# Two images on the 128 partitions and X as the stationary operand of the convolution, with the table's rows reordered by a permuted identity

## The reference, cut to what matters

```python
xn = (x - mean) / sqrt(var + 1e-5)                   # per image and channel
y = conv(xn, conv_w, padding=15, rhs_dilation=5)     # 32 channels -> 1, 7 x 7
imp = sigmoid(gelu(batchnorm(y + conv_b)))
xs = xn * imp
idx = sort(top_k(imp.reshape(B, -1), 192))           # pixels
tokens = xs[:, :, idx].T + make_pos[idx]
t1 = layernorm(tokens + attention(tokens, 8 heads))
t2 = layernorm(t1 + relu(t1 @ w1.T) @ w2.T)
xs[:, :, idx] = t2.T
return x + xs
```

## Time and profile before

| | us |
|---|---|
| median of 3 runs | 1159.79 |
| lowest, highest | 1157.36, 1163.17 |
| span of the profiled execution, first to last instruction | 1225.6 |

### The profile page before, as it was taken

How to read it: one execution, slowest core, us unless ns; L and a number is a source line. 1 busy time by engine, 2 the same in 40 slices (tenths; PEclk the granted TensorE clock), 3 DMA queues, 4 the chain that set the end, 5 groups by cost and what they waited for, 6 DMA issues and landing times.

```text
span 1225.6 us, 21628 instructions
## 1 busy us (share of the span) xinstructions
PE 971.3 (79%) x6440; PEld 762.4 (62%) x6440; DVE 835.0 (68%) x2114; ACT 774.3 (63%) x1899; POOL 631.8 (52%) x851
## 2 busy tenths in 40 slices
PE   3986865689888988898889889986786786488676
PEld 2765643577667766776678667865664565366544
DVE  5345776488558967896879677976694676455644
ACT  2545644486547786877688768875866575267543
POOL 4333316632665368546854576557516655562352
PEclk8998988799879999999899999998987589699855
DMA  9998977555566989898989888965453555436778
GB/s 244 314 264 227 272 210 180 146 159 157 133 156 184 266 217 237 236 291 208 233 238 274 228 238 227 265 187 143 132 169 98 132 154 151 123 98 195 212 221 269
DMA packets 176252, 247.82 MB, mean 202 GB/s; under 512 B 65512, under 2 KB 71912, under 8 KB 176136
## 3 DMA queue, kind: packets, MB, share of 16 engines
q1 hardware_dynamic: 167944, 244.03, 71.9%
q0 software_dynamic: 8192, 2.40, 1.5%
HBM read 124.53 MB, written 121.80 MB: 201 GB/s over the span
## 4 chain that ended last, share of the span: by engine, by line
PE 38%; DVE 20%; ACT 12%; issue 9%; DMA 9%; another core or an unknown queue 6%; POOL 5%; SPq 1%; ACTq 0%; DVEq 0%; POOLq 0%
PE cv L527 10%; PE sc L646 7%; PE pp L659 4%; PE xb L511 4%; PE tr L561 3%; DVE res L1350 3%; ACT wgt L843 3%; PE ib L574 2%; ACT pr L872 2%; PE ms L675 2%; DMA table<-xt 2%; DMA X<-in_x 2%; DVE stats L1126 2%; DMA tok_pos<-in_pos,idx 2%
## 5 line engine op out<-in xcount | busy, mean ns | idle before, releaser
L527 PE MATMUL cv<-X,w_conv 128*128 128x330 f32 (+1 forms) x1024 | 302.2, 422 | 11.6 <-issue 5.9
L527 PEld LDWEIGHTS cv<-X,w_conv 128*128 128x128 f32 x1024 | 193.3, 203 | 45.9 <-issue 12.1
L843 ACT ACTIVATE wgt<-ib,eps_col,mom 128x440 f32<-128x440 f32 (+1 forms) x256 | 177.6, 701 | 46.3 <-DVE res L1350 22.0
L1145 DVE TENSOR_SCALAR_CACHE_REDUCE junk<-flat,th 128x379 bf16<-128x379 f32 x200 | 120.6, 603 | 115.3 <-ACT th L829 89.3
L511 PE MATMUL xb<-cst,X 128*110 128x128 f32 x900 | 153.7, 297 | 48.8 <-ACT xt L809 28.3
L646 PE MATMUL sc<-k_b,qm 128*128 128x192 f32 x768 | 172.2, 353 | 16.2 <-DVE pixf L1245 7.3
L1046 POOL TENSOR_SCALAR res<-res,mom 128x440 f32<-128x440 f32 (+1 forms) x152 | 96.0, 634 | 171.0 <-DVE res L1350 169.3
L1350 DVE SCALAR_TENSOR_TENSOR res<-tr,mom,wgt 128x440 f32<-128x440 f32 (+1 forms) x192 | 122.2, 641 | 71.4 <-PE tr L561 31.0
L809 ACT COPY xt<-xb 110x512 f32<-110x512 f32 x225 | 131.6, 585 | 58.9 <-PE xb L511 30.7
L872 ACT ACTIVATE pr<-sc,least 128x192 f32<-128x192 f32 x384 | 137.1, 415 | 31.0 <-DVE least L1314 18.6
L659 PE MATMUL pp<-cst,pr 128*96 128x128 f32 x768 | 122.5, 284 | 33.6 <-ACT pt L883 25.4
(11 more groups left out here) (170 smaller groups left out, 1534.2 us busy)
## 6 DMA issues: line engine op xcount, KB each, us to landing
table<-xt SPq DMA_DIRECT2D x240, 224.0 KB
rt<-table SPq DMA_DIRECT2D x240, 224.0 KB
out<-res SPq DMA_DIRECT2D x320, 137.5 KB
X<-in_x SPq DMA_DIRECT2D x64, 412.5 KB, 6.4
X<-in_x SPq DMA_DIRECT2D x64, 343.8 KB, 6.5
conv_rows<-cvr SPq DMA_DIRECT2D x64, 188.0 KB
y<-conv_rows SPq DMA_DIRECT2D x64, 165.4 KB
out<-res SPq DMA_DIRECT2D x64, 68.8 KB
```

Of the source, the lines that this page charges most:

```text
L527: last = mm(cv[:, 0:CUT[half]], w_conv[:, 4 * q + z], X[:, m % XI, at0:at0 + CUT[half]], start=z == 0, stop=z == 3)
L843: last = A(wgt[:, n % 2, at0:at0 + w], ib[:, at0:at0 + w], ACT.Identity, scale=mom[:, NB * g + b, 2:3], bias=eps_col[:, 1:2])
```

## The change

Two images share the partitions: partition 64*b + 2*c + s holds channel c of image b, and of each ten rows of the image the five with s. A pair has 55 tiles without padding in 14 units (V), the last of three tiles; a group is two pairs, 28 units. Each load brings one block of five rows for all 128 partitions, 11 a pair; X holds three pairs. The transposes into the table take `halves_apart`, an identity with its columns permuted, as the moving operand, so that the rows come out with the two strips apart. The convolution makes a tile of X stationary and moves the taps: for each row r of five, 11 products with up to 2 x 7 x 8 columns add into one bank; ScalarE copies the 308 columns into zs with a stride of five. Seven products for each image with shifted identities then sum the taps, so DRAM, y7 and VectorE's sum are left out. Statistics need no move between partitions: two products with two columns each, one averaging the neighbouring partitions of a channel and one permuting the result, go through bank ib. The output ring has 8 blocks of five tiles, rt holds six units instead of seven. The slot constants are new. The rest of the layer is as before but for small moves in the order.

```diff
-    U = 30
-    RQ, BLKS, BW = 30, 6, 5 * H
-    XI, RT, RING = 4, 7, 40
+    PAIRS, TILES, BLKS, BW = 2, 55, 11, 5 * H
+    V = 14
+    U = PAIRS * V
+    XI, RT, RING = 3, 6, 8
-        LOAD, INTO, MOMENTS, NORMAL = -21, -11, -5, (-2, -1, -1)
-        TAPS, SUM = (10, 17, 25, 31), (15, 20, 28, 32)
-        GELU, IMP_OUT, FLAT, SEARCH, IMP_IN = 33, 35, 38, 40, 58
...
-        EMBED, PROJECT, SCORES = 82, 86, 87
-        MIX, NORM, FEED, NORM2 = 114, 115, 118, 120
-        SCATTER, BACK, IMPB = 122, 127, (123, 127, 135, 142)
+        LOAD, INTO, STATS, AVERAGE, TURN, NORMAL = -28, -15, -16, -4, 1, (-2, -1, 1, 3, 5)
+        LAST, GELU, IMP_OUT, FLAT, SEARCH, IMP_IN = 10, 26, 28, 31, 33, 51
...
+        EMBED, PROJECT, SCORES = 75, 79, 81
+        MIX, NORM, FEED, NORM2 = 108, 109, 111, 113
+        SCATTER, BACK, IMPB = 115, 120, (116, 120, 128, 134)
         SLOTS = range(INTO, U * G + BACK + 2)
...
+            if m >= XI and k == 0:
+                eng.wait_ge(conv_ok, upto(conv_ok, (m - XI) // PAIRS, 6 * ((m - XI) % PAIRS) + 4))
+            eng.dma_start(X[:, m % XI, BW * k:BW * k + BW], x_rows[m][:, :, k]).then_inc(x_in[m % XI][k >= CUT_IN], 16)
...
-                for r in range(4):
-                    b, k = divmod(4 * u + r, RQ)
-                    last = nc.tensor.transpose(bank[0:H, 128 * r:128 * r + 128], X[:, (NB * g + b) % XI, H * k:H * k + H], ident)
+                for r in range(count):
+                    k = first + r
+                    last = nc.tensor.transpose(bank[0:H, 128 * r:128 * r + 128], X[:, m % XI, H * k:H * k + H], halves_apart)
...
-                for z in range(first, last_z):
-                    blk_in = 2 * q + z
-                    pe.wait_ge(xn_ok, upto(xn_ok, g, 3 * b + blk_in // 2))
-                    at0 = BW * blk_in + CUT[0] * half
-                    last = mm(cv[:, 0:CUT[half]], w_conv[:, 4 * q + z],
-                              X[:, m % XI, at0:at0 + CUT[half]], start=z == 0, stop=z == 3)
+                bank = cv[0:H, 0:2 * ZC].rearrange("p (a t) -> p a t", t=TB)
+                for q in range(6, BLKS) if late else range(6):
+                    lo, hi = max(0, 2 * q - 3), min(TB, 2 * q + 5)
+                    at0 = H * (5 * q + r)
+                    last = mm(bank[:, :, lo:hi], X[:, m % XI, at0:at0 + H], w_conv[:, :, lo + 3 - 2 * q:hi + 3 - 2 * q],
+                              start=q == 0, stop=q == BLKS - 1, skip_group_check=True)
...
+            def conv_last(g, h, b):
+                if b == 0:
+                    pe.wait_ge(cv_cp, upto(cv_cp, g, 6 * h + 4))
+                for k in range(KS):
+                    last = mm(cv[0:H, H * b:H * b + H], zs[:, b, k, :], shift[:, 5 * k:5 * k + H], start=k == 0, stop=k == KS - 1)
...
+            def average(g, h):
+                pe.wait_ge(stat_ok, upto(stat_ok, g, h))
+                for sem, value in ib_read[-1:]:
+                    pe.wait_ge(sem, value)
+                ib_read.append((avg_rd, upto(avg_rd, g, h)))
+                mm(ib[:, MOM:MOM + 2], pair_avg, own_mom[:], start=True, stop=True).then_inc(avg_ok, 1)
...
+                for sem, value in ib_read[-1:]:
+                    pe.wait_ge(sem, value)
+                ib_read.append((wgt_ok, upto(wgt_ok, g, u)))
+                mm(ib[:, 0:H * count], bones[:], imp_b[:, H * first:H * (first + count)], start=True, stop=True).then_inc(ib_ok, 1)
...
+                if r < 5:
+                    nc.scalar.copy(zs[:].rearrange("p b k (t r) -> p (b k) t r", r=5)[:, :, :, r],
+                                   cv[0:H, 0:2 * ZC].rearrange("p (a t) -> p a t", t=TB)).then_inc(cv_cp, 1)
...
+                if r == 0:
+                    pool.wait_ge(var_ok, upto(var_ok, g, h))
+                    gp.tensor_tensor(mom[:, m, 2:3], mom[:, m, 4:5], eps_col[:, 0:1], ALU.pow).then_inc(rstd_ok, 1)
+                    pool.wait_ge(rstd_ok, upto(rstd_ok, g, h))
+                    pool.wait_ge(xt_tr, upto(xt_tr, g, V * h + V - 1))
+                v = X[:, m % XI, :].rearrange("p (q r j) -> p q r j", r=5, j=H)[:, :, r]
```

545 lines of the change are left out of this document (252 added, 293 removed).

## The result

The changed kernel takes 1150.11 us (median of 5 runs, 1148.57 to 1150.88) against 1159.79 of the kernel before beside it (5 runs): ratio 0.991, 95% interval 0.988 to 0.9939. That is 0.9% faster, where 4.8% was forecast.

What follows compares the result with a forecast made beforehand. It took DMA to bind the first 180 us, nearly full queues 480 to 840 us, fixed sequences 840 to 1140. Stage gains of 67 us and +8 of waits made 1225.6 into 1166.6, times 0.9463 = 1104 us; range 1052 to 1162.

Steps and rivals of the forecast that it cites:

- The frame: Whole slot list: 361 slots instead of 380, so if a slot costs the same, 5% of the time goes.
- -18 for about this stretch: 480 to 840 us, all stages running: TensorE 5% and the others 7 to 13% lighter, -18 us, bounds -14 and -40.
- 840 to 1140 us: Loads and convolution running out: fixed sequences set slot lengths, but there are fewer slots, -12 us.
- GpSimd "at 52% busy bounds no stretch": GpSimd, whole kernel: fewer columns normalised and some copies and powers gone, priced at nothing.
- TensorE: Convolution as 2208 records of 96 ns, fewer transposes, new averages: net -37 us, 4% of 971 busy.
- rival 3: Convolution records: stationary load not hidden, 187 instead of 96 ns each, slower at 1237 us; chance 0.13.
- VectorE and ScalarE: Busy time over the kernel: VectorE -88 of 835 us (11%), ScalarE -58 of 774 us (7.5%).
- Rival 2: 0 to 180 and 480 to 840 us: DMA binds more than held, 1072 us, or 1050; chance 0.20.
- the 18 taken for the first 180 us: 0 to 180 us, bound by DMA: fewer slots and less DMA traffic, -18 us, at most 31.
- New waits: Spreading waits for the averages' updates in a shared bank: 0.5 us for each of 16 pairs, +8 us, bounds 0 and +32.
- rival 4: Whole list: squeezed fixed work and new waits at their bound lengthen slots and pay back the shorter list, 1155 us; chance 0.15.
- Scaling by 0.9463: Final sum: profiled span of 1225.6 us scaled to the runs' median of 1159.79, turning 1166.6 into 1104 us.

Runs made afterwards that it cites:

- a_30: The changed kernel with each pair's 55 tiles cut into 15 units instead of 14, so 30 slots a group and 379 in all: 1148.76 us, 0.9887 of before.
- a_gath: The changed kernel without the eight gathers of positions in each group (zeros added instead): 1116.89 us, 0.9629 of before.
- a_pe: The changed kernel with six of the eleven products of each of the convolution's sums left out: 1128.04 us, 0.9703 of before.
- b_dve: The kernel before with VectorE's sum taken over one tap instead of seven: 1155.64 us, 0.9987 of before.
- a_zsplain: The changed kernel with ScalarE's copy into zs written without its stride, so the map's rows are permuted: 1146.23 us, 0.9909 of before.
- b_nodma: The kernel before without the convolution's round trip through DRAM and the waits for it: 1140.53 us, 0.9867 of before.
- a_noavg: The changed kernel without the two small products for the moments, each partition using its own statistics: 1145.29 us, 0.9872 of before.
- b_rt6: The kernel before with six instead of seven units read ahead on the way back (rt): 1161.88 us, 1.0021 of before.
- a_four: The changed kernel without position gathers, six of eleven convolution products, and most VectorE statistics of X, and with Exp for Gelu: 1045.4 us, 0.9019 of before.

## Why the prediction went wrong

**The frame was the step that failed**: "if a slot costs the same, 5% go". It fed nearly every line of the sum. A slot did not cost the same: from the first gather to the first way back it went from 3.43 to 3.73 us, in the full stretch from 3.99 to 4.39, in the emptying from 2.76 to 2.90. a_30 refutes the frame for the run as a whole: with 379 slots instead of 361 the kernel is no slower. It was wrong in its spread too, since between the first gather and the first way back no slot was saved at all, and these 53 slots took 16 us more; in a_30, at 30 slots a group, they take 11 us less than at 28. What is left at 30 slots in the full stretch, with 8% fewer tiles, is 119 us a group against 120: there the lighter tiles bought next to nothing. Squeezing the same work into 28 slots costs 3 to 4 us a group there, which is the 10 us of the table. The forecast had -18 for about this stretch. Only in the emptying does the frame have something, and half of it: 7 us were won where -12 was forecast for 840 to 1140 us and -3 for the last 85, and a_30 gives 15 us back with its 10 slots, 1.5 each where one takes 2.8.

**GpSimd "at 52% busy bounds no stretch", priced at nothing**, was the second. Its busy share leaves out the 0.30 us between gathers, and an average hides that they stand in one block of 24 for each group. They take 24 x 1.22 = 29.3 us in eight slots of three gathers, 3.66 us a slot, over the mean slot of before, 1155.9/380 = 3.04. The change made these eight slots no fewer, and longer: the block went from 32.0 to 35.5 us, as the steps of the new normalisation fall into it. What these 3.5 us cost was not tested by moving the steps; a_30, with 32.7 us, is faster by some 4 us a full group, but a_gath, with 28.6, is not, so they do not explain the full stretch by themselves. The timeline of GpSimd in the kernel before would have shown it; I read only its sum on the page. The Trainium skill, "Perfetto Trace Analysis", What "DMA-bound" means, lists the issuing engine's sequencer as a bound of its own, apart from the DMA engines; the runs without gathers agree in sense, with 33 to 39 us.

**TensorE.** Right in price. Timeline of the changed kernel, the sum over the taps:

```profile
504.32 1.52 PE L498 MATMUL cv<-cst,zs 110*110 110x110 f32 x14
505.68 0.38 PE L672 MATMUL ms<-cst,o_t 128*96 128x128 f32 x2
```

There are 2208 records, as forecast, and these 14 start in 505.68 - 504.32 = 1.36 us, 97 ns each, forecast 96. The 112-column records (L488) start 97 ns apart as well at full clock, by the median of 925. (At half clock it is 187, just the price of rival 3, so the clock has to be looked at before the spacing is read.) Rival 3 falls: load and stream overlap though both use nearly the whole array, and the rule of the Trainium skill ("TensorE: Matmul & The Clock Gate", The mechanism) that they overlap only across row groups, which would make it 187 ns, isn't borne out. (The same section also lets a load go ahead into the background weight buffer, and these rows would fit that.) Of its busy time 29 us went between the two unstretched profiles (939.7 to 910.6), where -37 of queue were forecast. What was wrong is what that is worth: at 26 of 100, as in a_pe, an estimate of 8 to 10 us. **The clock** had no term in the sum, and it fell: 0.90 instead of 0.93 to the first gather, 0.88 instead of 0.92 from there to the first way back, 0.892 instead of 0.905 over the run. TensorE's convolution leads the chain of the first two stretches, so a part of the 16 us lost may be the clock's; no run separates it.

**VectorE and ScalarE.** 765 us, forecast 745; 735, forecast 715. The aggregation fell to 7.7 us (6 forecast). The one price badly off is the strided copy into zs: 722 ns, not 410, which in 80 copies is 25 us, more than the 20 that ScalarE is over. But relief of either engine by itself is worth next to nothing: b_dve 0.1% for 36 us, a_zsplain nothing for 24.

**DMA.** 214.9 MB, forecast 216. (The KB of the rows are of 1024 bytes, so the round trip is 23.2 MB and not 22.6, as b_nodma shows; that makes the forecast 215.5.) Rival 2 (DMA binds more, 1072 us) was half right: in the first 180 us DMA was the largest part of the chain and left it, and the first gather comes 25 us sooner, between the 18 taken for the first 180 us and the bound of 31. b_nodma has 19 of the 25 by itself. But TensorE's convolution took its place there, at 30.3% of the chain, and in the full stretch the DMA share fell from 0.93 to 0.73 while a group became longer; b_nodma gains 4 us there. So DMA bound the filling in the main, up to the first gather, and more than half of that gain was lost again in the next 53 slots.

**New waits.** The view of waits, changed kernel: engine, line, released by, total us, times, longest.

```profile
DVE mom L1115 <- PE ib L510: 33.6, 10, 11.3
```

The spreading waits 9.9 us for `back` (L1127) and 5.7 for `mom` (L1119), 15.6 in all and over the 10 forecast, below the 30 of rival 4. GpSimd's power and normalisation were called covered by two slots; the convolution waits 14.4 us for them, less than in before (25.4 us), so that holds. a_noavg puts a price of 4 us on the averages, from nothing to 11 by its interval; +8 was forecast. VectorE's own 33.6 us (L1115) hardly matter as far as b_dve, an edit on the other kernel, tells what VectorE's time is worth.

**Rival 4** (longer slots pay the shorter list back, 1155 us, chance 0.15) is what happened, at 1150, by half its mechanism: not the new waits at their bound, but the fixed work of a group squeezed from 30 slots into 28, which a_30 undoes at 11 us from the first gather to the first way back and 11 in the full stretch. It was given too little because its counter-argument, "all engines get lighter per group", does not count for the full stretch, where they did and a group took 3 us more.

**Scaling by 0.9463** was an error by itself. The stretched profile made a slot 3.2 us instead of 3.04, so the 19 slots looked dearer; in per cent of the whole it cancels, and it didn't decide.

**The account**, by the ratios, each to about 4 us and the averages to 7: round trip out -15 (b_nodma), VectorE's sum -2 (b_dve), averages +4 (a_noavg), strided copy 0 (a_zsplain), smaller ring +2 (b_rt6), 28 slots instead of 30 +3 (a_30): -8. Measured is -10, so some -2 is left for 8% fewer tiles and the other form of the convolution together. With such intervals on six terms the rest may as well be ten less or ten more, and these were single edits on two different kernels, so they needn't add up. The account shows that no single part took the gain back; it does not prove the rest to be nothing.

**Still open.** Which pairs of engines make up the full slot was not taken apart: a_four shows that the four reliefs together shorten a group from 123 to 111 us, and the single ones to no less than 119.7. Of the 16 us lost between the first gather and the first way back, a_30 accounts for 11; the rest, and what the lower clock and the steps between the gathers have in it, is open. Why the first profile of before was stretched isn't known either.

## What to carry to other kernels

In a kernel whose engines march through one list of slots, don't price a slot: find what runs in order within the slots of each stage, on which engine, and forecast a gain only where the removed work is in that chain. Look at the timeline of an engine with DMA issues of its own, since a 50% busy share can hide a queue that is full for over 30 us in each group, and before putting new work on it see whether it falls into that block. Compare two schedules between events that both have, and by stage: a_30 looks like nothing on the whole, and its profile is 23 us shorter up to the emptying and 15 us longer in it. And when the bound work leaves a stage, name what is late next in the following stage before booking the gain: here 25 us won before the first gather were down to 10 at the first way back.

## What the runs showed of the hardware

- Gathers by indirect DMA that follow one another on GpSimd start 1.22 us apart: 0.92 us shown and 0.30 not, in both kernels (median 1.22 to 1.23 us in every group).
- ScalarE writes 308 columns five float32 apart in 722 ns and the same in order in 419. I had looked at the columns only. The Trainium skill, "SBUF — State Buffer", Door 1, says that accesses are fastest while they stay in one line of 16 bytes, four float32; a stride of five leaves it at each element, and the two rows agree in sense.
- TensorE loads 110 columns and streams up to 112 every 97 ns at full clock (187 at half), with a new stationary operand each time.
- One profiled execution was 5.7% longer than the median of the runs of the same kernel, 1225.6 against 1159.79 us, and 6% longer than a second one, 1155.9, at the same granted clock in the full stretch (0.96, and the second profile). Over the whole execution the clock was 0.884 against 0.905.
- Less work for TensorE came with a lower granted clock: a_pe, 93 us lighter, ran at 0.86 over the run where the changed kernel has 0.89.
